# Spread ids copied to SBUF by ScalarE, layers placed around the last pairs, and GpSimd taking the low-part subtractions, in a fused embedding and interaction kernel

## The reference, cut to what matters

```python
e = stack([tbl_f[ids[:, f]] for f in range(26)], axis=1)      # 2048 x 26 x 128, f32
combined = concatenate([e, r_dense_x[:, None, :]], axis=1)     # 2048 x 27 x 128
interact = einsum('bfd,bgd->bfg', combined, combined)
z = interact[:, TRIU_I, TRIU_J]                                # 351 pairs of each sample
h = concatenate([z, r_dense_x], axis=1)                        # 479 columns
h = maximum(h @ W_top1 + b_top1, 0.0)                          # 512
h = maximum(h @ W_top2 + b_top2, 0.0)                          # 256
y = h @ W_top3                                                 # 2048 x 1
```

## Time and profile before

| | us |
|---|---|
| runs of the kernel | 424.28, 424.46, 430.18 (median 424.46) |
| profiled execution, its own time | 428.22 |
| its span, first to last instruction | 426.1 |
| PE busy | 394.1 (92%) |
| POOL busy | 299.9 (70%) |
| DVE busy | 226.5 (53%) |
| ACT busy | 204.8 (48%) |

### The profile page before, as it was taken

One profiled execution on the slowest core, in us unless ns is written; L12 is line 12 of the kernel. 1 busy time (PEld: TensorE's weight loads), 2 busy tenths in 40 slices (PEclk: granted clock), 3 DMA queues, 4 the chain that ended last, 5 costly groups with the idle time before them and its releaser, 6 DMA issues. The chain is left out here.

```text
span 426.1 us, 5916 instructions
## 1 busy us (share of the span) xinstructions
PE 394.1 (92%) x2200; PEld 299.6 (70%) x2200; DVE 226.5 (53%) x459; ACT 204.8 (48%) x339; POOL 299.9 (70%) x296
## 2 busy tenths in 40 slices
PE   6999889999998999999998999999995999996896
PEld 2655449798887685968877675968774666696685
DVE  3999995685956370744935380834913141313040
ACT  2242425565636453635546443635645346654432
POOL 7777787477787777777877777777877777777000
PEclk9999999999999999999999999999998999999999
DMA  4467622222233223232322123231112222121000
GB/s 120 164 203 208 175 75 75 74 71 81 75 87 74 51 74 101 55 92 57 83 76 79 51 74 100 62 87 53 36 51 55 53 52 57 51 57 50 8 0 2
DMA packets 16740, 32.45 MB, mean 76 GB/s; under 512 B 6388, under 2 KB 7031, under 8 KB 16713
## 3 DMA queue, kind: packets, MB, share of 16 engines
q0 software_dynamic: 9216, 18.89, 17.4%
q1 hardware_dynamic: 7496, 13.19, 10.0%
HBM read 32.05 MB, written 0.01 MB: 75 GB/s over the span
## 5 line engine op out<-in xcount | busy, mean ns | idle before, releaser
L318 POOL DMA_INDIRECT gat<-in_tbl,idx x288 | 297.8, 1034 | 93.1 <-issue 87.5
L586 DVE COPY z<-gram 32x216 f32<-32x216 f32 x128 | 49.2, 384 | 179.7 <-PE gram L384 177.6
L384 PEld LDWEIGHTS gram<-ct 128*128 128x128 f32 x1024 | 118.5, 192 | 10.3 <-issue 6.5
L384 PE MATMUL gram<-ct 128*128 128x108 f32 x1024 | 119.8, 275 | 1.6 <-ACT ct L494 0.7
L357 PE MATMUL prod<-ring,tab_hi 125*128 125x512 f32 x256 | 108.8, 425 | 5.3 <-DVE ring L572 3.2
L359 PE MATMUL prod<-ring,tab_lo 125*128 125x512 f32 x256 | 101.8, 398 | 0.0
L578 DVE TENSOR_SCALAR ring<-idb,rowid 125x512 fp32r<-125x512 int32 x192 | 83.3, 493 | 1.4
L494 ACT COPY ct<-front 128x512 f32<-128x512 f32 (+1 forms) x80 | 75.0, 1000 | 3.4 <-PE front L345 2.6
L357 PEld LDWEIGHTS prod<-ring,tab_hi 125*128 125x128 f32 x256 | 49.0, 191 | 31.4 <-DVE ring L572 13.8
L502 ACT COPY z<-gram 32x216 f32<-32x216 f32 x128 | 42.1, 329 | 53.3 <-PE gram L384 52.1
L359 PEld LDWEIGHTS prod<-ring,tab_lo 125*128 125x128 f32 x256 | 49.2, 192 | 7.9
(11 more groups left out here) (55 smaller groups left out, 186.4 us busy)
## 6 DMA issues: line engine op xcount, KB each, us to landing
idb<-in_ids_t SPq DMA_DIRECT2D x24, 256.0 KB, 3.3
gat<-in_tbl,idx POOLq DMA_INDIRECT x288, 2.6
oh<-in_tbl SPq DMA_DIRECT2D x3, 500.0 KB
oh<-in_dense_t SPq DMA_DIRECT2D x4, 256.0 KB, 3.2
gat<-in_tbl SPq DMA_DIRECT2D x2, 500.0 KB
h<-in_tbl SPq DMA_DIRECT2D x2, 500.0 KB
w1z<-in_w SPq DMA_DIRECT2D x1, 702.0 KB
w2s<-in_w SPq DMA_DIRECT2D x1, 512.0 KB
```

The costliest lines, as they stand in the source:

```text
L318: nc.gpsimd.indirect_dma_start(out=gat[:, t % GS, i, :], out_offset=None, in_=tables[f][:, :], in_offset=bass.IndirectOffsetOnAxis(ap=idx[ ...
L384: ins = nc.tensor.matmul(gram[:, c % 2, i, 0:SPG * NF].rearrange("p (j f) -> p j f", j=SPG), four.rearrange("p j f -> p (j f)"), four[:, : ...
L586: ins = nc.vector.tensor_copy(z1[QUAD * j:QUAD * (j + 1), c * CG:(c + 1) * CG, :], gram[QUAD * j:QUAD * (j + 1), c % 2, :, NF * j:NF * (j ...
```

## The change

Three edits.

ACT copies each spread field of block 0 from PSUM to one of three places in SBUF (`ids_homes`: two halves of `h2`, one third of `zt`), and DVE builds the ring from there. The first three copies stand at the head of ACT's list, ahead of the first two high-part casts; the other five follow the copy of the products of fields 0 to 4.

`split_low` moves from DVE to POOL: after gather 3, 5, 7, ... 17 of tile 0 POOL subtracts the low part of field 0, 1, 2, ... 7, each with a wait for that field's high part.

In tile 15's steps the four first-layer blocks of job 4 (tile 14) go behind the gram chunks, out of the gaps between the transposes; job 4's second layer goes behind the pairs of tile 15, and its third layer ahead of the tail's second layer. The tail uses other PSUM banks.

```diff
     if t == TILES - 1:
-        return T[0:1] + Z + T[1:2] + N[4:6] + T[2:3] + N[6:7] + E[0:2] + T[3:4] + E[2:4] + T[4:5] + G + E[4:]
+        return T[0:1] + Z + T[1:2] + N[4:6] + T[2:3] + N[6:7] + T[3:5] + G + E[0:4]
...
                         ).then_inc(gathered[t % GS][c], 16)
+                        if t == 0 and i >= 3 and i % 2 == 1:
+                            split_low((i - 3) // 2)
+
+            def split_low(m):
+                pool.wait_ge(hi_ready, m + 1)
+                nc.gpsimd.tensor_sub(tab_lo[0:OH_P, m, :, :].rearrange("p k d -> p (k d)"), raw_table(m),
+                                     tab_hi[0:OH_P, m, :, :].rearrange("p k d -> p (k d)")).then_inc(lo_ready, 1)
...
             turn_pairs(TILES - 1)
-            pe.wait_ge(back_free, len(BACK_INDEX))
-            pe.wait_ge(prod_free, NO * NB + len(PROD_INDEX))
+            layer_step(NB, 2, 0)
+            layer_step(NB, 2, 1)
+            pe.wait_ge(back_free, BACK_INDEX[("Z", TILES - 1)] + 1)
             for i, (_, n, m) in enumerate(TAIL):
+                if (n, m) == (2, 0):
+                    layer_step(NB, 3, 0)
...
+            def copy_spread(m):
+                act.wait_ge(spread, m + 1)
+                if m >= 3:
+                    act.wait_ge(built, OH_K * (m - 2))
+                nc.scalar.copy(ids_homes[m % 3], spread_ids(m)).then_inc(spread_copied, 1)
+
+            for m in range(3):
+                copy_spread(m)
             split_high(0)
             split_high(1)
...
                         copy_products(*q)
+                        if q[0] == 0 and q[1] + 3 < NO:
+                            copy_spread(q[1] + 3)
                         if q[0] == 0 and q[1] + 2 < NO:
                             split_high(q[1] + 2)
...
-            def split_low(m):
-                dve.wait_ge(hi_ready, m + 1)
-                nc.vector.tensor_sub(tab_lo[0:OH_P, m, :, :].rearrange("p k d -> p (k d)"), raw_table(m),
-                                     tab_hi[0:OH_P, m, :, :].rearrange("p k d -> p (k d)")).then_inc(lo_ready, 1)
-
...
-                        dve.wait_ge(spread, m + 1)
+                        dve.wait_ge(spread_copied, m + 1)
...
-                    nc.vector.tensor_scalar(ring[0:OH_P, k, :], spread_ids(m)[0:OH_P, :], rowid[0:OH_P, k:k + 1], None,
+                    nc.vector.tensor_scalar(ring[0:OH_P, k, :], ids_homes[m % 3][0:OH_P, :], rowid[0:OH_P, k:k + 1], None,
                                             ALU.is_equal).then_inc(built, 1)
...
             for m in range(NO):
-                split_low(m)
                 for k in range(OH_K):
                     build_chunk(0, m, k)
```

More of the change, by code:

```diff
@@ L117, in beside @@
     return step[0] == "L" and step[1] >= NB - 2 and step[3] % 2 == 1
+END = [("Z", TILES - 1), ("L", NB, 2, 0), ("L", NB, 2, 1), ("L", NB, 3, 0)]
+TAIL = [("L", 1, m) for m in range(M1)] + [("L", 2, m) for m in range(M2)] + [("L", 3, 0)]
 def bank_uses():
-    steps = [s for t in range(TILES) for s in tile_steps(t) if s[0] in "ZL"] + [("Z", TILES - 1)]
+    steps = [s for t in range(TILES) for s in tile_steps(t) if s[0] in "ZL"] + END
     return [s for s in steps if not beside(s)], [s for s in steps if beside(s)]
 BACK_INDEX, PROD_INDEX = [{s: i for i, s in enumerate(uses)} for uses in bank_uses()]
-TAIL = [("L", 1, m) for m in range(M1)] + [("L", 2, m) for m in range(M2)] + [("L", 3, 0)]
 def onehots_of(t):
@@ L179, in build @@
         back = psum("back", [P, SB])
-        tail_banks = [back[:, :], prod[:, :]] + [front[:, i, :, :].rearrange("p f s -> p (f s)") for i in range(2)]
+        tail_banks = [front[:, i, :, :].rearrange("p f s -> p (f s)") for i in range(2)]
         tail_banks += [gram[:, i, 4 * k:4 * k + 4, :].rearrange("p g s -> p (g s)") for i in range(2) for k in range(2)]
+        tail_banks += [front[:, 0, 1:TCH, :].rearrange("p f s -> p (f s)")]
         ids_in = sem("ids_in")
@@ L186, in build @@
         spread = sem("spread")
+        spread_copied = sem("spread_copied")
         ids_rest_in = sem("ids_rest_in")
@@ L365, in spread_field @@
                 if m >= 4:
-                    pe.wait_ge(built, OH_K * (m - 3))
+                    pe.wait_ge(spread_copied, m - 3)
                 nc.tensor.matmul(spread_ids(m), pick_row[:, m, :], id_rows_f, start=True, stop=True).then_inc(spread, 1)
@@ L371, in gram_chunk @@
                 if n < 4:
-                    pe.wait_ge(built, OH_K * NO)
+                    pe.wait_ge(spread_copied, NO)
                 if c == 0:
@@ L430, in layer_block, with layer_step @@
                 return ins
+            def layer_step(job, n, m):
+                if (job, n, m) == (0, 1, 0):
+                    pe.wait_ge(weights_in, 16 * 6)
+                bank_clear(("L", job, n, m))
+                if m == 0:
+                    inputs_ready(job, n)
+                if beside(("L", job, n, m)):
+                    layer_block(prod, JOBS[job], n, m).then_inc(beside_done, 1)
+                else:
+                    layer_block(back, JOBS[job], n, m).then_inc(back_done, 1)
             pe.wait_ge(ident_ready, 1)
@@ L525, in finish_block, with finish_step @@
                         act.nop(nofuse=True).then_inc(free, 1)
+            def finish_step(job, n, m):
+                if (job, n, m) == (0, 1, 0):
+                    act.wait_ge(weights_in, 16 * 6)
+                if beside(("L", job, n, m)):
+                    act.wait_ge(beside_done, PROD_INDEX[("L", job, n, m)] + 1)
+                    finish_block(prod, JOBS[job], job, n, m, prod_free)
+                else:
+                    act.wait_ge(back_done, BACK_INDEX[("L", job, n, m)] + 1)
+                    finish_block(back, JOBS[job], job, n, m, back_free)
+            def copy_spread(m):
[5 more added lines that the diff above has]
+                copy_spread(m)
             split_high(0)
@@ L543, in _ @@
                     elif kind == "L":
[L544 to L552, removed]
+                        finish_step(*q)
             copy_pairs(TILES - 1)
+            finish_step(NB, 2, 0)
+            finish_step(NB, 2, 1)
             for i, (_, n, m) in enumerate(TAIL):
+                if (n, m) == (2, 0):
+                    finish_step(NB, 3, 0)
                 act.wait_ge(tail_done, i + 1)
```

16 lines of the change are left out of this document (4 added, 12 removed).

## The result

| | before | after |
|---|---|---|
| median, us | 424.37 (423.84 to 430.18, 4 runs) | 446.61 (445.46 to 447.06, 4 runs) |
| profiled execution: its time, span | 428.22, 426.1 | 447.06, 445.3 |
| PE busy | 394.1 | 391.3 |
| POOL busy | 299.9 | 316.6 |
| DVE busy | 226.5 | 215.8 |

The ratio is 1.0498, with a 95% interval of 1.0461 to 1.0534: 22.2 us slower by the medians. DVE and PE have a little less to do, POOL has 16.7 us more, and the span between the two profiled executions grew by 19.2. The medians and ranges in this document are over all executions, while the ratios, taken from the record, leave out single executions over 1.5% above the fastest of their kernel, so a ratio need not be the quotient of two medians.

A forecast was written before the change was run, and what follows sets the result against it. POOL's full gather stream was taken as a second bound as long as PE's chain. A stream delay of 22.6 us less 1.5 in the tail gives +21.1 on the median of 424.5: 445.6 us, range 433 to 457.

The forecast's parts named there:

- the tail: Tile 15: gram products start 3.5 us earlier, 1.8 and 0.15 us are given back, net -1.5 us.
- the walk: Tile 0, times added field by field up to tile 1's first gather: 55.0 us, ends 50.0 and 64.5, before 27.13.
- field 0: Tile 0: its products end at 20.3 us, the first high-part cast coming only after ACT's third copy.
- fields 1 to 5: Tile 0: these fields take 6.1 us each, between 5.1 and 8.0.
- The stream as second chain: POOL: 288 gathers at 1.25 us, 360 us, form a full chain as long as PE's.
- No slack left: Tiles 12 and 14: gathers come exactly in time; PE waits for them three times, 3.5 us in all.
- The subtraction's price: POOL in tile 0: 2.3 us for each low-part subtraction, 18.4 for eight; lower bound 1.1 each.
- The last step: End of tile 0's fields: copy, cast, hand-over and POOL's last subtraction take 4.2 us before the remaining gathers.
- a shut port: Tile 0: DVE's ring builds from SBUF shut POOL out; a third of the 3.2 us a field was taken.
- The lock-out rival: Tile 0: no gap in DVE's builds lets POOL in, 8.0 us a field, 455 us; chance 0.2.
- The lengthening left as it is: Later gathers: DVE's builds still lengthen them by 25.6 us over the kernel, 6 us allowed either way.
- D: POOL's gather stream and so PE at tile 14 are late by 22.6 us: 27.9 less 5.3 of absorbed wait.

The follow-up runs named there:

- Experiment 3: The kernel before with only the change's third edit, tile 14's layers placed around tile 15's pairs: 422.38 us, ratio 0.9947.
- experiment 4: The kernel before with 30 small subtractions of 128 elements put on POOL ahead of tile 4's first gather: 437.38 us, ratio 1.0288.
- experiment 7: The changed kernel with one gather of 18 left out in each of tiles 2 to 15, run three times: ratios 0.9689, 0.9742 and 1.0178.
- experiment 1: The kernel before with only the eight low-part subtractions moved to POOL, ring still built from PSUM: 446.42 us, ratio 1.0441.
- experiments 2: The changed kernel with the eight subtractions back on DVE, the rest as changed: 423.25 us, ratio 0.9885.
- experiment 9: The changed kernel, subtractions back on DVE, plus a one-element DVE memset behind every second ring build in blocks 1 to 3: ratios 0.9692 and 0.9823.
- experiment 6: The changed kernel with tile 0's transposes of chunks 3 and 4 moved behind field 7's products: 640.00 us against 638.08, ratio 1.0023.
- experiment 5: The changed kernel with POOL's eight subtractions cut to 16 of 1024 elements a lane, PE using the high part twice: 638.29 us against 638.08, ratio 1.0001.
- 8: The kernel before with one gather of 18 left out in each of tiles 2 to 15: 621.67 us, ratio 0.9765.

## Why the prediction was right

The forecast was 445.6, the median 446.6. Between the two profiled executions the terms of the sum came out at 20.6 (forecast 22.6) for the stream and -1.4 (forecast -1.5) for the tail, 19.2 together, as the spans show. Against the medians the loss is 22.2: the profiled execution of the kernel before was 3.8 us over its own median, and that of the changed kernel only 0.5. Experiment 3's trace, of an execution of usual length, shows where the 3.8 lay: its stream ends 3.75 us earlier, and against it the changed kernel's is 24.3 us later, 1.7 more than forecast. So an agreement within 1 us is partly luck: inside the walk, 2.6 us too much for field 0 and 4.5 too little for fields 1 to 5 partly cancelled.

*The stream as second chain.* Confirmed by experiment 4 (15.5 us in, 13.3 at the last gather, 12.8 out) and, less firmly, by experiment 7 from the other side (14 gathers fewer, about 14 us less, by ratios from two chips). The traces agree: from the last gather's end to the end of the span it is 32.3, 32.5 and 32.9 us with the old tail (the kernel before, experiments 1 and 4) and 30.9, 31.6, 31.9 and 30.4 with the new one (the changed kernel, experiments 2, 9 and 3), wherever the stream ends between 385 and 414. Only with gathers left out is it longer, 38.7. "No slack left" was read from one execution; it holds for the usual one too, where the weights of tile 14's last chunk wait 0.3 us for their gather (experiment 3).

*The subtraction's price.* 2.34 to 2.40 us, one 2.68; I took 2.3 from the affine select.

*The walk to tile 1's first gather.* 56.98 for 55.0, but its parts were further off. Field 0 ended at 17.7, not 20.3: I had ACT's first three copies hold up the first cast. They did not, because the spread matmuls got faster: four took 2.04 us where the same four fields had been eight rows and 7.16 us. With the ids' new place their operands had moved from f32 into fp32r tiles, and I read that edit as a change of address only. That the type is the reason was not tested alone. Against it, fields 1 to 5 took 7.0 us each and not 6.1. The last step, copy, cast and subtraction, was 4.16 for 4.2.

*Why 7.0.* Not the reason I priced. I set a third of DVE's build time on top for a shut port. The gathers of tile 0 are lengthened by 2.8 us in all, so the gaps between DVE's builds did let POOL in, and experiment 1, with no such build, reaches nearly the same point (55.2). The true surcharge is two waits that the walk lacked: PE for gathers 14 and 15 (4.5 us, and half clock behind it), which experiment 6 took away, 4.9 us of 57.0; and PE for ring slots in field 3 (1.9 us). The latter is the lock the other way round, a build from SBUF held until POOL's subtraction ended. Three controls bear it out: with such builds and full subtractions PE waits there 1.9 us (the changed kernel, experiments 6 and 7), and it doesn't with builds from PSUM (1), with subtractions on DVE (2) or with subtractions of 16 elements (5). So a size that came out about right had the wrong cause: the prediction priced DVE keeping POOL out, and what cost time in tile 0 was POOL keeping DVE out and PE waiting for gathers on their way.

*The lock-out rival* (455, chance 0.2) is refuted for tile 0 and for the reason given against it: DVE's builds there wait for PE. Where they don't wait, the lock is real, and experiment 9 shows that a 0.06 us instruction breaks it. The rule of the Trainium skill ("SBUF — State Buffer", Who interferes with whom) speaks of one instruction at a time; the earlier trace rows show a gather kept out over a whole gapless run of them, and tile 0 shows that waits in between let it in.

*The lengthening left as it is.* From tile 1 on 19.8 us; in the kernel before 24.3 in its profiled execution and 20.4 in experiment 3's. Against the first, this 4.5 is most of why D was 20.6 although the walk ended 2 us late; against the second the term was right.

*The tail.* Right in mechanism and size within the trace; alone it gave 2.2 us.

## What to carry to other kernels

An engine that issues DMAs is full when its issues follow each other at their own pitch, whatever its busy share says; set their number times the pitch against the span before giving it work, and look for waits of the consumer. What hurts most when work is moved into such a list is not the work but its waits: three quarters of the delay here came from the semaphore ahead of each subtraction, which tied a stream that had run ahead freely to the pace of the engine that it feeds. A gather issued late also shows its whole way to landing, 5.5 us here, which had been hidden before. If two chains are nearly equally long, a gain on one (9 us in tile 0) is worth what the other leaves, here 1 to 2%.

## What the runs showed of the hardware

- A run of VectorE builds from SBUF without a gap holds a GpSimd gather until the run ends (5.24 us beside 16 builds), while beside builds broken by a memset of one element every second build it takes at most 1.34 us (experiment 9), and beside builds paced by a semaphore at most 1.28 in tile 0 of the changed kernel and at most 1.93 in experiment 9's tiles 0 and 1. I had taken the lock for a matter of whether the two overlap; it is a matter of gaps.
- The same holds the other way round. In tile 0 of the changed kernel six of VectorE's builds from SBUF took 1.69 to 3.21 us, where most take 0.47, each beside a GpSimd subtraction of 1024 elements and ended 0.3 us behind it. Builds from PSUM beside the same subtractions took 0.75 at most (experiment 1).
- Thirty GpSimd subtractions of 128 elements, each waiting for the last, took 15.57 us, 0.52 each, while one of 1024 elements takes 2.35: on a straight line through these two the fixed part, with the wait, is about 0.26 us, an estimate.
- Chips differ by half for the same kernel: 424 to 430 us on some, 638 on two. On these the granted clock is 0.81 to 0.84, and PE is idle for about 100 us in pauses that the trace puts to nothing (53.4 and 37.3 us ahead of two kinds of matmul in experiment 5). Experiments 7, 8 and 9 are 2.4 to 3.1% faster than the kernel before there, experiments 5 and 6 are not. The cause is open.
